# Projections in units of 24 products between the attention tiles, blocks of the input streamed back in, output projection as a stage of its own

## What is computed

```python
def _masked_attention(xf, Wq, Wk, Wv, lookahead):
    q = jnp.einsum('bnd,hed->bhne', xf, Wq)      # k, v likewise
    s = jnp.einsum('bhqe,bhke->bhqk', q, k) * scale
    mask = i[:, None] <= i[None, :] if lookahead else i[:, None] >= i[None, :]
    p = jax.nn.softmax(jnp.where(mask, s, jnp.finfo(s.dtype).min), axis=-1)
    return jnp.einsum('bhqk,bhke->bhqe', p, v)
...
o = jnp.concatenate([o_lb, o_la], axis=1).reshape(B, T * F, D)   # not transposed back
out = jnp.einsum('bnd,od->bno', o, Wo).reshape(B, T, F, D)
x = x + _L0_conv_ref(_gn(x), ...)
```

## Time and profile before

| | us |
|---|---|
| median of 3 runs | 3385.69 |
| the profiled execution's own time | 3385.93 |
| its span, first to last instruction | 3383.9 |
| TensorE busy | 3176.5 (94%) |
| VectorE busy | 2068.3 (61%) |
| ScalarE busy | 1740.5 (51%) |
| GpSimd busy | 1672.6 (49%) |

### The profile page before, as it was taken

How to read it: one execution, slowest core, us unless ns; L and a number is a source line. 1 busy time by engine, 2 the same in 40 slices (tenths; PEclk the granted TensorE clock), 3 DMA queues, 4 the chain that set the end, 5 groups by cost and what they waited for, 6 DMA issues and landing times.

```text
span 3383.9 us, 50389 instructions
## 1 busy us (share of the span) xinstructions
PE 3176.5 (94%) x14472; PEld 2494.5 (74%) x14472; DVE 2068.3 (61%) x3454; ACT 1740.5 (51%) x3525; POOL 1672.6 (49%) x1306
## 2 busy tenths in 40 slices
PE   4999998999999679999999999999999999999998
PEld 3888887788888457777777777777777777777776
DVE  6212111310110488888888888888888888888885
ACT  2100110210100267777767777777777777777774
POOL 2000000100000367777777777777777777777774
PEclk9999999999999789999999999999999999999999
DMA  6325223422311222111112111212121112111210
GB/s 236 100 84 137 93 66 82 154 71 50 97 62 48 65 83 62 59 55 44 56 50 69 44 56 50 69 44 57 51 69 44 51 56 68 45 50 57 64 37 19
DMA packets 142546, 232.91 MB, mean 69 GB/s; under 512 B 76800, under 2 KB 76800, under 8 KB 142336
## 3 DMA queue, kind: packets, MB, share of 16 engines
q1 hardware_dynamic: 142336, 230.73, 22.8%
HBM read 163.58 MB, written 67.11 MB: 68 GB/s over the span
## 4 chain that ended last, share of the span: by engine, by line
PE 28%; POOL 13%; DVE 12%; issue 9%; ACT 1%; DMA 1%; POOLq 0%; DVEq 0%; SPq 0%; ACTq 0%
POOL p_low L690 6%; POOL k L715 4%; PE acc L1059 4%; PE acc L1063 4%; PE max L1015 4%; PE acc L1061 4%; PE scores L1045 4%; PE rows L1077 3%; PE scores L1040 3%; DVE o_full L984 3%; DVE part_max L930 2%; POOL q L711 2%; DVE p_low L690 2%; DVE diagonal L701 1%; PE side L1025 1%
## 5 line engine op out<-in xcount | busy, mean ns | idle before, releaser
L690 POOL TENSOR_TENSOR p_low<-probs,p_high 128x512 fp32r<-128x512 f32 (+2 forms) x960 | 1190.9, 1258 | 573.8 <-ACT p_high L863 539.9
L859 ACT ACTIVATE probs<-scores 128x512 f32<-128x512 f32 (+3 forms) x1280 | 684.3, 535 | 410.0 <-PE scores L1045 383.6
L930 DVE TENSOR_REDUCE part_max<-max 128x1 f32<-128x512 f32 (+3 forms) x1280 | 766.1, 603 | 197.8 <-PE max L1015 175.8
L863 ACT ACTIVATE p_high<-scores 128x512 fp32r<-128x512 f32 (+3 forms) x1280 | 683.4, 534 | 0.0
L1015 PE MATMUL max<-k,q 128*128 128x512 f32 (+3 forms) x1280 | 489.5, 383 | 72.6 <-DVE part_max L930 36.0
L1059 PE MATMUL acc<-p_high,v 128*128 128x512 f32 (+3 forms) x1280 | 477.6, 373 | 28.3 <-POOL p_low L690 20.1
L318 DVE COPY stage_d<-proj 128x512 f32<-128x512 f32 x96 | 66.0, 690 | 710.9 <-PE proj L264 462.7
L1040 PE MATMUL scores<-q,k 128*128 128x512 f32 (+3 forms) x1280 | 478.0, 373 | 11.9 <-ACT p_high L863 8.9
L1045 PE MATMUL scores<-q,k 128*128 128x512 f32 (+3 forms) x1280 | 489.0, 382 | 0.0
L1063 PE MATMUL acc<-p_low,v 128*128 128x512 f32 (+3 forms) x1280 | 469.0, 366 | 0.0
L1061 PE MATMUL acc<-p_high,v 128*65 128x512 f32 (+3 forms) x1280 | 462.2, 361 | 0.0
(11 more groups left out here) (96 smaller groups left out, 5083.5 us busy)
## 6 DMA issues: line engine op xcount, KB each, us to landing
raw<-qk_s SPq DMA_DIRECT2D x256, 256.0 KB, 4.2
xs<-xT SPq DMA_DIRECT2D x64, 512.0 KB, 5.0
w_raw<-wqk SPq DMA_DIRECT2D x32, 512.0 KB, 3.7
qk_s<-stage_a SPq DMA_DIRECT2D x64, 256.0 KB, 2.4
qk_s<-stage_d SPq DMA_DIRECT2D x64, 256.0 KB, 2.4
raw<-v_s SPq DMA_DIRECT2D x64, 256.0 KB, 2.8
res<-x_res SPq DMA_DIRECT2D x32, 512.0 KB, 4.4
out<-res SPq DMA_DIRECT2D x32, 512.0 KB, 2.6
```

Source lines behind the costliest of these rows:

```text
L690: eng.tensor_tensor(p_low[:, n % 4, part], probs[:, n % 4, part], p_high[:, n % 4, part].bitcast(F32), ALU.subtract).then_inc(done, 1)
L859: nc.scalar.activation(probs[:, n % 4, 0:cols], scores[n % 2][:, 0:cols], ACT.Exp, scale=SCALE).then_inc(exp_done, 1)
L863: nc.scalar.activation(p_high[:, n % 4, 0:cols], scores[n % 2][:, 0:cols], ACT.Exp, scale=SCALE).then_inc(high_act, 1)
L930: nc.vector.tensor_reduce(part_max[:, s % 2, at, m:m + 1], max_bank[n % 2][:, 0:cols], AX.X, ALU.max).then_inc(max_read, 1)
```

## The change

The program now has three stages.

**`begin`** does batch one only: statistics, normalising and splitting as before. It makes q and k of the first pair of heads (8 tiles), v of all eight heads of the first kind (16 tiles) and q and k of the second pair (8 tiles): 32 tiles, 768 products of 512 columns. It also stores x's two halves to HBM (`xh_s`, `xl_s`), in blocks of 256 tokens.

**`attend`** makes the rest. x comes back in blocks of 256 tokens, two in SBUF at a time. A unit is one block of one pair of heads and one of q, k, v: 24 products of 256 columns into one of two spare banks. Pairs 2 and 3 have 16 units each, pairs 4 to 15 have 24 (v is turned: units give it as channels x tokens, so ScalarE copies it out, TensorE transposes it in two products, ScalarE copies again): 320 units, 7680 products. Four units stand in the prologue; the rest go into slots two heads ahead of the pair that needs them, all 24 products of one in one slot. The last two pairs of heads have no units. ScalarE copies a unit out in the next slot. The weights of a pair are loaded and split at the pair's start (ScalarE high, GpSimd low, slots -1, 1 and 5; 1024 columns each). The second batch is counted from slot 80 on and normalised from slot 172 on, in 32 pieces of 512 columns, and stored. There is no loop on the engines; a head's output is stored to `o_s`.

**`finish`** loads Wo and the 32 heads' outputs, splits them, makes 64 x 24 products of 512 columns and adds x.

```diff
--- before.py
+++ after.py
-def project(nc, xT, wqk, wv, qk_s, v_s):
+def begin(nc, xT, wqkv, wv, xh_s, xl_s, qk_s, v_s):
...
+            def store_x(h):
+
+                sp.wait_ge((x_low_pool, x_low_dve)[h % 2], h // 2 + 1)
+                first = (h % 2) * NBLK // 2
+                for part, kept in ((xh, xh_s), (xl, xl_s)):
+                    sp.dma_start(kept[0, first:first + NBLK // 2, :, h // 2, :].rearrange("k p t -> p k t"),
+                                 part[:, h // 2, (h % 2) * HALF:(h % 2 + 1) * HALF].bitcast(F32)
+                                 ).then_inc(x_stored, 16)
...
+            for h in range(X_UNITS):
+                load_x(1, h)
+                if h >= X_SLOTS:
+                    store_x(h - X_SLOTS)
...
-OP_SLOT = {0: 9, 1: 10, 2: 11, 3: 15, 4: 16, 5: 17}
-ADD_SLOT = {0: 13, 1: 19}
...
+LEAD = 2
+FILLED = PAIRS - LEAD
+V_EARLY = KIND_PAIRS
+PRODUCTS = 3 * NC
+PRO_UNITS = 4
...
+def units():
+
+    return [(pair, block, c) for pair in range(LEAD, PAIRS) for block in range(NBLK)
+            for c in range(3 if pair >= V_EARLY else 2)]
...
+    for pair in range(LEAD, PAIRS):
+        own = [u for u, unit in enumerate(every) if unit[0] == pair and u >= PRO_UNITS]
+        base, products = (pair - LEAD) * 2 * SLOTS, PRODUCTS * len(own)
+        for m, u in enumerate(own):
+            slot = base + (2 * m + 1) * PRODUCTS * SLOTS // products
+            put(slot, "unit", u, 0, PRODUCTS)
+            finish[u] = slot
+    for u, slot in finish.items():
+        put(slot + 1, "evict", u)
+        put(slot + 2, "keep", u)
+        if every[u][2] == 2:
+            put(slot + 3, "turn", u)
+            put(slot + 4, "turned out", u)
+            put(slot + 5, "keep turned", u)
+    for n, (pair, block) in enumerate(blocks[2:]):
+        last = max(u for u, unit in enumerate(every) if unit[:2] == blocks[n])
+        put(finish.get(last, -1) + 1, "x load", n + 2)
+    for w, (pair, c) in enumerate(weight_sets()):
+        if pair > LEAD:
+            base = (pair - LEAD) * 2 * SLOTS
+            load, high = ((-12, -4), (-2, 0), (2, 4))[c]
+            put(base + load, "w load", w)
+            put(base + high, "w high", w)
+            put(base + high + 1, "w low", w)
...
+                elif step == "unit":
+                    u, k0, k1_ = h, n, k
+                    pair, part, c = every[u]
+                    b = blocks.index((pair, part))
+                    if k0 == 0:
+                        pe.wait_ge(w_low, sets.index((pair, c)) + 1)
+                        pe.wait_ge(x_loaded[b % 2], 32 * (b // 2 + 1))
+
+                        to = spare_bank("unit", u)
+                    else:
+                        to = spare[home["unit", u][0]]
+                    products = [(ch, w, x) for ch in range(NC) for w, x in ((wh, xh), (wh, xl), (wl, xh))]
+                    for m in range(k0, k1_):
+                        ch, w, x = products[m]
+                        last = nc.tensor.matmul(to[:, 0:BLK], w[:, c, ch, :],
+                                                x[:, b % 2, ch, :], start=(m == 0), stop=(m == PRODUCTS - 1))
+                    if k1_ == PRODUCTS:
+                        last.then_inc(filled, 1)
+                elif step == "turn":
+                    pe.wait_ge(evicted, h + 1)
+                    to = spare_bank("turn", h)
+                    for t in range(2):
+                        last = nc.tensor.transpose(to[:, t * P:(t + 1) * P], v_flat[:, t * P:(t + 1) * P], eye_f[:, :])
+                    last.then_inc(v_turned, 1)
...
+def finish(nc, x_res, wo, o_s, out):
...
-def build(nc, xT, x_res, wqk, wv, wo, qk_s, v_s, out):
-    project(nc, xT, wqk, wv, qk_s, v_s)
-    attend(nc, x_res, wo, qk_s, v_s, out)
+def build(nc, xT, x_res, wqkv, wv, wo, xh_s, xl_s, qk_s, v_s, o_s, out):
+    begin(nc, xT, wqkv, wv, xh_s, xl_s, qk_s, v_s)
+    attend(nc, xT, wqkv, xh_s, xl_s, qk_s, v_s, o_s)
+    finish(nc, x_res, wo, o_s, out)
```

More of the change, by code:

```diff
@@ L107, in project, with x_unit @@
         stored_d = [sem(f"stored_d{n}") for n in range(2)]
[L109 to L136, removed]
+        def x_unit(again, h):
+            return again * X_UNITS + h
         block = ctx.enter_context(nc.Block())
@@ L166, in _ @@
             for h in range(X_UNITS):
[L167 to L199, removed]
@@ L423 @@
+            low_x(dve, X_UNITS - 1, x_low_dve)
+            weights_and_tiles(dve, False)
 STAGES = T // NQ
@@ L514, in slots @@
                 if at == t and has_next:
[L515 to L525 removed]
+                    plan.append((step, h + 1, n))
@@ L526, in slots @@
+        plan += [step for step in filling if step[0] not in LEAVING]
+        plan.append(("values", h, t))
     return plan
 def prologue():
[L531 to L537 removed]
@@ new lines, in prologue, with homes @@
+    plan += [("scores", 0, t) for t in range(AHEAD)]
+    plan += [("evict", u), ("keep", u)]
+    return plan
+def homes(steps):
+    home, left, owner, summing = {}, [-1, -1], [None, None], None
+    for at, (step, *which) in enumerate(steps):
+        if step not in ("unit", "shift", "turn", "gn mean", "gn spread"):
+            continue
+        key = (step, *which[:2]) if step == "shift" else (step, which[0])
+        if key not in home:
+            bank = min((n for n in range(2) if n != summing), key=left.__getitem__)
+            home[key] = bank, owner[bank]
+            owner[bank] = key
+        bank = home[key][0]
+        left[bank] = at
+        if step == "unit":
+            summing = None if which[2] == PRODUCTS else bank
+    return home
@@ new lines, in attend, with steps @@
+        gn_kept = sem("gn_kept")
+        every = units()
+        sets = weight_sets()
+        turns = [u for u, unit in enumerate(every) if unit[2] == 2]
+        stores = [u for u, unit in enumerate(every) if unit[2] < 2]
+        blocks = []
+        for unit in every:
+            if not blocks or blocks[-1] != unit[:2]:
+                blocks.append(unit[:2])
+        def steps():
+            yield from prologue()
+            for h in range(G_HEADS):
+                yield from slots(h)
+            for step in ("leave", "invert", "spread", "divide", "store"):
+                yield (step, G_HEADS - 1, 3)
@@ L780, in _, with wait_kept @@
+            def wait_kept(pair):
+                own = [m for m, u in enumerate(stores) if every[u][0] <= pair]
+                for slot in range(2):
+                    sp.wait_ge(kept_out[slot], 16 * sum(m % 2 == slot for m in own))
+                own = [u for u in turns if every[u][0] <= pair]
+                reached(sp, v_out, 16 * len(own))
+            for step in steps():
+                do(*step)
+            sp.wait_ge(o_stored, 16 * G_HEADS)
         @block.gpsimd
         def _(pool):
-            nc.gpsimd.memset(probs[:, 0, 0 * P:1 * P], 0.0).then_inc(eye_made, 1)
```

1174 lines of the change are left out of this document (708 added, 466 removed).

## The result

The changed kernel takes 3574.7 us in the median (3572.6 to 3578.4) beside 3386.7 for the kernel before on the same chip (3383.3 to 3388.7): ratio 1.056, 95% interval 1.054 to 1.058. It is 188 us slower. The forecast was 3340, with 0.26 on slower and a range up to 3432; the time lies 235 us above the one and 143 above the other.

The account below looks back on a forecast made before the run. It took TensorE to bound the projection, and heads to stall where other engines have more work. Stages up to the first value product (294.4 us), heads, and output stage summed to 3338.3, plus 2.0 outside the span: 3340 us, range 3262 to 3432.

Parts of the forecast that it names:

- The stall of a head with units: Heads 4 to 27, 12 units each: TensorE stalls 5.2 us a head, ends 2.2 and 8.9.
- my floor of 2.2: Lower end of the stall in a head with 12 units: 2.2 us, the floor of waits alone; chance of stall gone 0.18.
- The rival on GpSimd at the joint: Weights' low halves on GpSimd delay a pair's first slots: at most 95 us, 3435; GpSimd or another engine behind units 0.23.
- The turns: Heads 4 to 27: four turns of V a head, 0.5 us each (0.12 to 1.3), 2.0 a head.
- The units' pace: Inside a unit, products of 256 columns start 0.117 us apart, so 24 products take 2.81 us.
- The pace of the weight load: Rival: each unit product runs at its 0.19 us load, 540 us more, 3880 in all; chance 0.02.
- The bare heads: Heads 28 to 30, without units or output projection: 60.5 us each (56.5 to 67), VectorE setting the pace in slots 9 to 17.
- The second batch: Heads 2 to 8: its statistics and normalising run beside the units at no cost.
- Heads 0 to 3: Heads 0 and 1 with six units take 71.7 us each, heads 2 and 3 with eight take 76.4 each.
- The prologue: Stretch before the heads, 28.9 us at half clock: four units and two weight splits add 5 us (0 to 12).
- begin with the stores: First stage: storing both halves of x behind its second pass adds 12 us, ends 0 and 35.
- the output stage: Last stage: 12 us of opening, then 1536 products at 0.2266 us, 348.1 us; whole stage 371.0.

Follow-up runs that it names:

- the weights' chain: Changed kernel with a pair's three weight loads and high halves moved to earlier slots, nothing else: 3501.2 us, 73 us back.
- the bank of the shift: Changed kernel with the shift product of slot 32 moved to slot 34, nothing else: 3506.7 us, 68 us back.
- the three edits: Changed kernel with weight steps earlier, one shift in slot 34 and half of the next head's q, k, v low halves on VectorE: 3400.6 us.
- the third buffer: Changed kernel with three instead of two raw slots for the next head's q, k, v, and earlier loads: 3564.8 us.

## Why the prediction was wrong

**The stall of a head with units** is the step that failed: 5.2 us a head forecast, 13.8 measured (96.3 less 82.5 of work at full clock), 206 us more over 24 heads. I had worked out the 5.2 by setting TensorE's work against VectorE's busy time in four parts of a head, and took the 8.9 us of now as its upper end. But a stall is set by who is waited for, and the change brought new waits. Shown by the experiments: the weights' chain 73 us and the bank of the shift 68. Half of the next head's low halves on VectorE gives 30 us and leaving out the second batch 30, but both mostly in heads 4 to 9; they may be largely the same time, and no run takes both. The rest of the 206 us is not assigned. With the three edits the stall is still 6.8 us a head, and my floor of 2.2 had no room for the small differences between products, 4.6 us a head here and 5.3 before.

The rival on GpSimd at the joint had the place (first slots of a pair, low halves of weights) and came near the price (95 us at most, 73 measured), but had the wrong mechanism: it added up busy times, 22.9 against 22.2, with one low half in slot -1 that really stands in slot -3. The trace shows GpSimd busy 18.8 of 30.5 us, and a single buffer with load, rounding and subtraction one behind the other. By the rival's breakeven of 1.9 us a head the 3.1 of this hole alone decide the sign of the forecast.

**The turns** I put at 0.5 us each. One form of it in after:

```profile
L1186 PE MATMUL spare<-eye_f,v_flat x192: 270/272/274, 669.3 to 2945.3; 128*128 128x128 f32 x192
```

From start to start the two products of a turn lie 0.108 us apart, and the next work follows 0.03 us behind: 0.14 in all, at the low end of my 0.12 to 1.3. That saved 35 us of the forecast and hid as much of the stall. The figure that the prediction took from the Trainium skill, "TensorE: Matmul & The Clock Gate", section "Part 4: PE-mode transpose" (about 275 ns, for a bf16 transpose of 128 x 128 in a kernel), is near the drawn duration of one here, 272 ns, and 2.5 times the distance of two.

**The units' pace** held: 0.120 us in the median and 0.117 for one in ten, for 0.117 forecast; the difference is 23 us over 7680 products. It stands among the 13.8 us as 0.9 a head. The pace of the weight load (0.19) never shows. The fixed 2.5 ns a product that the Trainium skill has in "TensorE: Matmul & The Clock Gate", section "Wait — 56ns, not 53.3ns?", is too small here: 256 columns / 2.4 GHz is 106.7 ns, so the part beyond the columns is 10 to 13 ns.

**The bare heads**: 67.8 us each for 60.5. I took VectorE's 16.8 us for the bound of slots 9 to 17, by busy time again. The waits name the chain of loads and splits (GpSimd is busy 17.3 of 23.0 us in that window), and the kernel before had it as well, hidden right behind the output projection. So moving 10.9 us out of a head gave nothing where nothing was put in its place: 67.8 is even above my upper end of 67. The old kernel without most of the output projection shows that TensorE's work is not the bound there. That the chain alone is the bound is not shown: the third buffer took 2.8 us from a bare head and the low halves on VectorE 1.2, and then VectorE's own work held it, so no version came below 65.0.

**The second batch** was booked at nothing and measured at 30 us. VectorE's mean load left room; that its pieces stand in line before maxima and low parts is my reading, and no run parts them. **Heads 0 to 3** (+32) are mostly something else: without the second batch they lose 5 us, without the blocks' loads 9, and the rest is open. **The prologue** took 36.6 us and not 33.9, the set-up 27.2 for 20.7: more transfers (278 GB/s for 134). Only noted from the windows, not tested.

**Right**: begin with the stores at 12 us, a choice between 0 and 35 that came out (12.9; no run tests its reason), and the output stage (375.6 for 371). In this one two errors partly cancel: the opening took 14.3 us from the last value product to the first of Wo, for 16.2 forecast, and the products of Wo 357.3 for 351.1.

```profile
3200.76 0.27 PE L1162 MATMUL acc<-p_low,v 128*128 128x128 f32 x1
3215.01 0.77 PE L1345 MATMUL rows<-wo_h,o_high 128*128 128x512 f32 x1 [13.98 <-DVE o_low L1286]
```

What stays open: the best version is 16 us behind the kernel before (3400.6 beside 3384.9 on the same chip). The bare heads and heads 0 to 8 hold more than that over the forecast, but no run closed their holes.

## What to carry to other kernels

Before moving work out of a loop or into it, ask what each wait of the bound engine would become: a wait that recurs in every round with a tiny length can mark a chain that arrives just behind it, and here it took over as soon as the work ahead of it went. For added work list the resources that are held, not only engine time: the raw buffer (load, rounding, subtraction and next load form one serial chain) and the PSUM banks (who holds them in the slot in which another step asks). And hand such steps slots by the length of the chain; here one line of slot numbers was worth 73 us and a single one 68. And before gains are added, look where in the program each of them lies: a hole closed in every round gave nothing in most of them.

## What the hardware showed that I had not expected

- The granted clock fell to half within a hole of 2.7 us in a head, though TensorE was busy 24.5 of 30.5 us around it, and stayed there through a second hole of 2.2 us and the first 18 products of the next unit. In heads 4 to 27 products at half clock cost 1.9 us a head on top of 7.3 of holes, a quarter more.
- Leaving out 1176 products lowered the mean clock of 1909 us from 1.00 to 0.95: of the 9.5 us of products freed a head, products at half clock took back 2.5.
- Two full float32 transposes of 128 columns start 0.108 us apart, though each is drawn 0.272 us long.
